# Attention and FFN block on one core: three rounded matmuls a product against one fp32 matmul

## The reference

```python
n  = layernorm(x)
q  = rope((n @ Wq).reshape(b, n, 32, 8)); k, v = split(ctx @ Wkv); k = rope(k)
x  = x + softmax(q @ k.T / sqrt(8)) @ v @ Wout + bout
h  = layernorm(x)
route = sum of the two largest of (h @ gate_w)          # 8 columns
y  = relu(h @ up_w)**2 @ down_w + (h @ expert_weight) * route
out = x + (layernorm(y) * gamma + beta)
```

## Time and profile before

| | us |
|---|---|
| median of 3 runs | 251.4 |
| lowest and highest run | 251.2, 253.0 |
| span of the profiled execution | 250.5 |
| TensorE matmuls busy in it | 221.1, 1754 records |
| VectorE, ScalarE, GpSimd busy | 167.7, 141.3, 105.3 |

### The profile page before, as it was taken

One profiled execution on the slowest core, in us unless ns is written; L12 is line 12 of the kernel. 1 busy time (PEld: TensorE's weight loads), 2 busy tenths in 40 slices (PEclk: granted clock), 3 DMA queues, 4 the chain that ended last, 5 costly groups with the idle time before them and its releaser, 6 DMA issues.

```text
span 250.5 us, 4919 instructions
## 1 busy us (share of the span) xinstructions
PE 221.1 (88%) x1754; PEld 175.5 (70%) x1754; DVE 167.7 (67%) x374; ACT 141.3 (56%) x284; POOL 105.3 (42%) x129
## 2 busy tenths in 40 slices
PE   2959768899999999999998999998889999778980
PEld 1847535677777787879786878877557886567980
DVE  6965899868886789684559974745998100572455
ACT  3256457597767675865647667564446967111520
POOL 7774566731238014474653136231324454332003
PEclk9995799999999999999999999999999999955896
DMA  7943141102101101010101110101000000000001
GB/s 199 357 94 84 47 107 45 28 20 62 48 24 29 42 3 48 0 48 0 47 0 43 46 47 0 46 3 44 0 27 21 5 0 3 0 0 22 3 21 42
DMA packets 12743, 10.68 MB, mean 43 GB/s; under 512 B 2992, under 2 KB 12336, under 8 KB 12720
## 3 DMA queue, kind: packets, MB, share of 16 engines
q1 hardware_dynamic: 11680, 10.37, 14.7%
q10 hardware_dynamic: 1040, 0.01, 0.2%
HBM read 5.13 MB, written 1.05 MB: 25 GB/s over the span
## 4 chain that ended last, share of the span: by engine, by line
PE 68%; DVE 18%; issue 6%; ACT 3%; POOL 2%; DMA 1%; POOLq 0%; DVEq 0%; ACTq 0%
PE ps_bg L956 18%; PE ps_bg L939 11%; PE ps_st L1037 11%; PE ps_o L1053 10%; PE ps_s L1021 9%; PE ps_dn L1109 9%; DVE mneg L837 7%; DVE stats L702 2%; DVE mnat L844 1%; PE ps_st L972 1%; DMA pos_sb<-in_fside_BxSx 1%; DVE mnat L845 1%; DVE by_token L710 1%; ACT kmask L612 1%; DVE rot_c L766 1%
## 5 line engine op out<-in xcount | busy, mean ns | idle before, releaser
L837 DVE TENSOR_REDUCE mneg<-ps_s 128x2 f32<-128x512 f32 x128 | 84.6, 684 | 36.4 <-PE ps_s L1021 35.7
L641 ACT ACTIVATE probs<-ps_st 128x512 f32<-128x512 f32 x128 | 73.3, 595 | 26.4 <-PE ps_st L1037 26.1
L1037 PE MATMUL ps_st<-qstack,kmask 128*128 128x256 f32 x256 | 57.3, 308 | 0.5 <-ACT probs L641 0.4
L1021 PE MATMUL ps_s<-kmask,qstack 128*128 128x512 f32 x128 | 54.4, 428 | 3.1 <-DVE mneg L837 1.9
L1037 PEld LDWEIGHTS ps_st<-qstack,kmask 128*128 128x128 f32 x256 | 39.9, 189 | 15.1 <-issue 9.5
L473 POOL TENSOR_SCALAR var_eps<-mv 128x1 f32<-128x1 f32 (+1 forms) x20 | 7.1, 353 | 75.0 <-DVE mv L705 74.9
L1053 PE MATMUL ps_o<-probs,vaug 128*32 128x256 f32 x512 | 34.3, 385 | 0.0
L1021 PEld LDWEIGHTS ps_s<-kmask,qstack 128*128 128x128 f32 x128 | 25.1, 197 | 7.2 <-DVE mneg L837 5.2
L956 PE MATMUL ps_bg<-x2nT,up 128*128 128x256 f32 x192 | 27.3, 296 | 1.0 <-ACT x2nT L573 1.0
L956 PEld LDWEIGHTS ps_bg<-x2nT,up 128*128 128x128 f32 x192 | 26.1, 202 | 2.0 <-ACT moe L672 1.4
L1109 PE MATMUL ps_dn<-down,inner 128*128 128x256 f32 x192 | 25.4, 283 | 0.2 <-DVE inner L341 0.2
(11 more groups left out here) (109 smaller groups left out, 311.5 us busy)
## 6 DMA issues: line engine op xcount, KB each, us to landing
kmask<-kstack SPq DMA_DIRECT2D x60, 64.0 KB, 2.1
x_sb<-in_x SPq DMA_DIRECT2D x4, 256.0 KB, 6.6
whole<-in_L_ffn_down_w SPq DMA_DIRECT2D x4, 256.0 KB, 5.4
qstack<-mT SPq DMA_DIRECT2D x64, 4.0 KB
result<-y_fin SPq DMA_DIRECT2D x8, 128.0 KB, 1.7
c_sb<-in_ctx SPq DMA_DIRECT2D x4, 128.0 KB, 2.4
oT<-in_L_ffn_up_w SPq DMA_DIRECT2D x1, 512.0 KB, 5.5
y_fin<-in_L_ffn_up_w SPq DMA_DIRECT2D x1, 512.0 KB, 7.4
```

The source lines that it names most:

```text
L641: act.activation(probs[n % 2][:, i, :, :], ps_st[k % NST][:].rearrange("p (t n) -> p t n", t=T), ACT.Exp, scale=SCALE).then_inc(st_free, 1)
L837: dve.tensor_reduce(mneg[m % 2][:, t, n % 2, 2 * half:2 * half + 2], ps_s[(4 * n + k) % NS][:].rearrange("p (i k) -> p i k", i=2), AX.X, A ...
L1021: pe.matmul(ps_s[(4 * n + k) % NS][:], qstack[b % 2][:, g, t * P:(t + 1) * P], kmask[:, g, 2 * half:2 * half + 2, :], start=True, stop=Tru ...
L1037: ins = pe.matmul(ps_st[k % NST][:, t * N:(t + 1) * N], kmask[:, g, i, t * P:(t + 1) * P], qstack[b % 2][:, g, :], start=True, stop=True)
```

## The change

Every product with weights is made of single fp32 matmuls on the operands themselves. All high and low parts go, with the operations that make them and the semaphores between; the copies out of the banks are ScalarE's alone and write fp32 once. The square writes `inner` directly. Weights are loaded straight into their tiles, all at the start, and the first use of each on TensorE waits for its load. The list, its slots and the warm-ups stay. Scores and PV stay as they are.

```diff
-        wkv = sb("wkv", [P, 2, 1, 2 * D], f32r)
-        wout = sb("wout", [P, 2, KC, D], f32r)
-        up = sb("up", [P, 2, KC, F], f32r)
-        expert = sb("expert", [P, 2, KC, D + E], f32r)
-        down = sb("down", [P, 2, FT, D], f32r)
+        wq = sb("wq", [P, KC, D])
+        wkv = sb("wkv", [P, 1, 2 * D])
+        wout = sb("wout", [P, KC, D])
+        up = sb("up", [P, KC, F])
+        expert = sb("expert", [P, KC, D + E])
+        down = sb("down", [P, FT, D])
         bout_sb = sb("bout_sb", [P, D])
...
@@ -325,20 +308,11 @@
 
 
 
-        def squares(eng, e, j):
+        def squares(eng, b, j):
+            taken(eng, (f"up{j}", b))
+            inner_read(eng, b, j)
             h = whole[j % HB][:]
-            if e == ("up0", B - 1):
-                eng.wait_ge(h_ready, 4 * (B - 1))
-            taken(eng, e)
-            eng.tensor_tensor(h, h, h, ALU.mult).then_inc(square_ready, 1)
-
-        def lo_squares(eng, b, j):
-            k = 4 * b + j
-            eng.wait_ge(square_ready, k + 1)
-            eng.wait_ge(h_hi_ready, k + 1)
-            hi, lo = (inner[:, j % 2, part, :, :] for part in range(2))
-            inner_read(eng, b, j)
-            eng.tensor_tensor(lo, whole[j % HB][:], hi.bitcast(f32), ALU.subtract).then_inc(h_ready, 1)
+            eng.tensor_tensor(inner[:, j % 2, :, :], h, h, ALU.mult).then_inc(h_ready, 1)
 
...
@@ -382,38 +337,27 @@
                 ring = slice(b % 2 * T, (b % 2 + 1) * T)
                 sp.dma_start(c_sb[:, ring, :], cv[:, b * T:(b + 1) * T, :]).then_inc(ld_c[b], 16)
 
-            def load_down(j):
-                sp.dma_start(whole[j % HB][:], by_rows(down_w)[:, 2 * j:2 * j + 2, :]).then_inc(ld_down[j % HB], 16)
-
             def load_tokens(b):
                 tiles = slice(b * T, (b + 1) * T)
                 if b < 2:
                     load_context(b)
                 if b == 0:
-                    sp.dma_start(raw_kv, Wkv).then_inc(ld_wkv, 16)
+                    sp.dma_start(wkv[:, 0, :], Wkv).then_inc(ld_wkv, 16)
                 sp.dma_start(x_sb[:, tiles, :], xv[:, tiles, :]).then_inc(ld_x[b], 16)
 
             load_tokens(0)
-            sp.dma_start(raw_q, by_rows(Wq)).then_inc(ld_wq, 16)
+            sp.dma_start(wq[:], by_rows(Wq)).then_inc(ld_wq, 16)
             load_tokens(1)
-            for k in range(KC):
-                sp.dma_start(raw_up[k], up_w[k * P:(k + 1) * P, :]).then_inc(ld_up, 16)
-            sp.dma_start(raw_out[:], by_rows(Wout)).then_inc(ld_wout, 16)
-            for j in range(HB):
-                load_down(j)
+            sp.dma_start(wout[:], by_rows(Wout)).then_inc(ld_wout, 16)
+            sp.dma_start(expert[:, :, 0:D], by_rows(expert_w)).then_inc(ld_expert, 16)
+            sp.dma_start(expert[:, :, D:D + E], by_rows(gate_w)).then_inc(ld_expert, 16)
+            sp.dma_start(up[:], by_rows(up_w)).then_inc(ld_up, 16)
+            sp.dma_start(down[:], by_rows(down_w)).then_inc(ld_down, 16)
             for b in range(2, B):
                 load_tokens(b)
             for v, t in ((bout, bout_sb), (gamma, gamma_sb), (beta, beta_sb)):
                 sp.dma_start(t[:], v.rearrange("(a d) -> a d", a=1).broadcast_to((P, D))).then_inc(ld_vec, 16)
             for e in ORDER:
-                while later_loads and e[0] == "S" and 4 * e[1] + e[2] >= later_loads[0][0]:
-                    _, which, split, count = later_loads.pop(0)
-                    sp.wait_ge(split, count)
-                    if which == "expert":
-                        sp.dma_start(raw_expert[:, :, 0:D], by_rows(expert_w)).then_inc(ld_expert, 16)
-                        sp.dma_start(raw_expert[:, :, D:D + E], by_rows(gate_w)).then_inc(ld_expert, 16)
-                    else:
-                        load_down(which)
                 if e[0] == "V" and e[1] + 2 < B:
                     sp.wait_ge(bg_full, full(("cT", e[1])))
...
@@ -525,19 +461,9 @@
                     xv = x_sb[:, b * T:(b + 1) * T, :]
                     pool.tensor_tensor(xv, xv, beta_sb[:].unsqueeze(1).broadcast_to((P, T, D)), ALU.add)\
                         .then_inc(x2b_ready, 1)
-                elif piece_at(e) is not None:
-                    i = piece_at(e)
-                    raw, parts, _, done = PIECES[i]
-                    pool.wait_ge(piece_hi, i + 1)
-                    pool.tensor_tensor(parts(1), raw, parts(0).bitcast(f32), ALU.subtract)\
-                        .then_inc(done, 1)
-                elif what[:2] == "up":
-                    j = int(what[2])
-                    if b < B - 1:
-                        squares(pool, e, j)
                 elif what[0] == "h":
                     if b < B - 1:
...
@@ -773,38 +668,15 @@
                 before = [by_token_uses(t)[by_token_uses(t).index(e) - 1] for t in range(T) if e in by_token_uses(t)]
                 bg_read(dve, *before)
 
-            def lo_part(e, parts, tokens=slice(0, N)):
-
-                hi, lo = (parts[:, part, :, tokens] for part in range(2))
-                dve.wait_ge(hi_ready, SPLIT[e] + 1)
-                of = bg(e)[:, 0:hi.shape[1] * hi.shape[2]].rearrange("p (k n) -> p k n", n=hi.shape[2])
-                emptied(dve.tensor_tensor(lo, of, hi.bitcast(f32), ALU.subtract), e)
-
             for e in ORDER:
                 what, b = e[0], e[1]
                 if what == "cT":
-                    if b >= 1:
-                        dve.wait_ge(bg_full, full(("V", b - 1)))
-                    else:
+                    if b == 0:
                         angles_in_turns()
-                    lo_part(e, cT)
                 elif what == "xT":
-                    if b >= 1:
-                        dve.wait_ge(bg_full, full(("Q", b - 1)))
-                    lo_part(e, xnT)
                     if b == 0:
                         taken(dve, ("K", b))
                         stack_rows(dve, link, 0, b)
-                elif what[:2] == "aT":
-                    t = int(what[2])
-                    if b >= 1:
-                        bg_read(dve, (f"W{t}", b - 1))
-                    lo_part(e, attnT, slice(t * P, (t + 1) * P))
-                elif what[:3] == "x2T":
-                    t = int(what[3])
-                    if b >= 1:
-                        bg_read(dve, ("E1", b - 1), ("up3", b - 1))
-                    lo_part(e, x2nT, slice(t * P, (t + 1) * P))
                 elif what == "ln1a":
                     dve.wait_ge(ld_x[b], 16)
                     if b >= 1:
...
@@ -940,29 +808,21 @@
                     at += m
                 ins.then_inc(bg_full, 1)
 
-            def split_product(to, lhs, rhs, fresh):
-
-
-
-                of, in_rhs = fresh
-                early, late = (((0, 0), (1, 0)), (0, 1)) if in_rhs else (((0, 0), (0, 1)), (1, 0))
-                terms = [(k, a, b_) for k in range(len(lhs)) for a, b_ in early]
-                terms += [(k, *late) for k in range(len(lhs))]
-                for c, (k, a, b_) in enumerate(terms):
-                    if c == 0:
-                        pe.wait_ge(hi_ready, SPLIT[of] + 1)
-                    if (a, b_) == late and k == 0:
+            def product(to, lhs, rhs, of):
+
+                for k in range(len(lhs)):
+                    if k == 0:
                         taken(pe, of)
-                    ins = pe.matmul(to, lhs[k][a], rhs[k][b_], start=(c == 0), stop=(c == len(terms) - 1))
+                    ins = pe.matmul(to, lhs[k], rhs[k], start=(k == 0), stop=(k == len(lhs) - 1))
                 return ins
 
-            def split_by_token(e, lhs, rhs, kc, cols, fresh):
+            def product_by_token(e, lhs, rhs, kc, cols, of):
 
                 begin(e)
                 for t in range(T):
-                    ins = split_product(bg(e)[:, t * D:(t + 1) * D],
-                                        [[lhs[:, a, k, t * P:(t + 1) * P] for a in range(2)] for k in range(kc)],
-                                        [[rhs[:, a, k, cols] for a in range(2)] for k in range(kc)], (fresh, False))
+                    ins = product(bg(e)[:, t * D:(t + 1) * D],
+                                  [lhs[:, k, t * P:(t + 1) * P] for k in range(kc)],
+                                  [rhs[:, k, cols] for k in range(kc)], of)
                 ins.then_inc(bg_full, 1)
 
             def keep_warm(count):
...
@@ -1067,32 +927,33 @@
                 elif what[0] == "W":
                     t = int(what[1])
                     if b == 0:
-                        pe.wait_ge(weights_split, WS)
+                        pe.wait_ge(ld_wout, 16)
                     begin(e)
-                    split_product(bg(e)[:, 0:D],
-                                  [[attnT[:, a, k, t * P:(t + 1) * P] for a in range(2)] for k in range(KC)],
-                                  [[wout[:, a, k, :] for a in range(2)] for k in range(KC)],
-                                  ((f"aT{t}", b), False)).then_inc(bg_full, 1)
+                    product(bg(e)[:, 0:D],
```

(75 more changed lines are left out.)

64 lines of the change are left out of this document (16 added, 48 removed).

## The result

The changed kernel takes 259.5 us (259.1 to 259.8) against 251.3 before (248.3 to 253.0). The ratio, between executions of comparable clock, is 1.037, interval 1.027 to 1.046. It is slower, as forecast (261.0, range 255 to 266). The runs of the kernel before spread by 5 us, those of the changed one by 1; TensorE's clock in the last batch is a part of the reason and its clock in the start another, as the experiments show.

A forecast was written before the change was run, and what follows sets the result against it. TensorE's queue was taken as the bound from 45 to 216 us, latencies outside it. The terms 7.1 - 0.6 + 3.2 = +9.7 took the span from 250.5 to 260.2, plus 0.9 gave 261 us, range 255 to 266.

The forecast's parts named there:

- Price of a product: On TensorE, 256 columns: 0.434 us as fp32 against 0.355 as three rounded matmuls, +0.079 at full clock.
- The two ends of the bounds: Limits on a product's price on TensorE: 0.236 us (-0.119 each) up to 0.65 us (+0.30 each).
- rival 2: Faster: at full array width fp32 records stream like rounded ones, 0.236 us a product, about 235 us in all; chance 0.07.
- rival 3: Weight loads on TensorE not hidden: +0.30 us on each of 141 products, +42, near 300 us; chance 0.03.
- (a): 45 to 216 us: 141 products cost +11.1 us, less 4.0 for waits and empty time on TensorE, sum +7.1.
- rival 1: Absorbed: TensorE's empty time and the other engines' relief take most of the cost; +3.4, 254.8 us; chance 0.17.
- (b): 0 to 45 us: dearer first products against low parts and weight pieces dropped; sum -0.6, between -2.5 and +1.
- So that is worth 0: Start: first K product ready about 2 us sooner, counted as no gain because the chain runs over the tokens.
- Rival 4: Start: the clock's rise near 11 us comes a stretch later, slowing Q and fifteen warm-ups; +3.3, 264.5 us; chance 0.07.
- (c): 216 us to the end: dearer products sum to +3.85, taken as +3.2 because the clock might rise earlier.
- From span to time: End of the sum: measured time taken as 0.9 us above the span, so 260.2 became 261.1.
- The signs named: Profile checks: 192 TensorE records fewer, spacing 0.217, VectorE 14 us less busy, ScalarE 17, GpSimd 31, attention 7 later, tail 37.

The follow-up runs named there:

- the repeated run: The changed kernel run again with no edit, for comparison on the same chip as the follow-up kernels: 259.4 us, ratio 1.039 to the kernel before.
- price-only kernel: Kernel before with each three-term product made one fp32 matmul on the high parts, low parts still made and waited for but unused: 264.0 us, ratio 1.046.

## Why the prediction was right, and where it was off

The direction and the mechanism are as forecast: TensorE was the full engine and pays more per product.

- Price of a product: 0.079 forecast, 0.077 measured (0.432 less 0.355). The two ends of the bounds are both out: full width streams no faster than the strips of L1053 (rival 2), and the weight loads stay hidden (rival 3). Of the two rules of the Trainium skill weighed there, the four passes of FP8 and Floating Point Precision, TensorE Precision Notes, are the one that these records bear out: a product is 0.432 / 0.118 = 3.7 times a rounded matmul. The 0.43 there isn't four times the rounded spacing at full clock, which would be 0.47; it is four times half of the 0.213 at the low clock.
- (a) The middle: +7.1 forecast, from 11.1 of price and 4.0 off; +7.0 measured, from 10.5 and 3.5 off. The terms are each 0.5 to 0.6 too large and cancel. What the relief took off was in good part empty time (5.1 to 2.9 us); with the helpers as before 1.0 us of the price did vanish, a small part of what rival 1 needs: it had +3.4 in all, and the times are 8.2 apart.
- (b) The start: -0.6 forecast, +1.1 measured in the profile (-0.2 in the repeated run, -0.5 in the changed kernel with tail warm-ups, whose start is the same). The step that failed is the one that puts the first weights' subtractions on GpSimd at nothing, "So that is worth 0": the subtraction for Wq, which it doesn't name, kept the memset away from VectorE's short operations, and without it these took 1.59 and 1.94 us and the tokens came later. With the memset moved the start gains 1.5 (by the medians) to 3.4 us (in the profile), so the relief was sized too small as well. That the forecast of -0.6 lies among the measured ones is luck: a relief too small and a stall left out. Rival 4 came in part: the spacing of the records fell to that of the full clock near 15.4 us, not near 11.1, the tokens' transposes having started 1.5 us later, and Q's eight records took 2.83 us (the windows give a granted clock of 1.00 there all the while, so this is read from the spacing alone); by 46 us most of that was made up.
- (c) The tail: +3.2 forecast, -1.2 measured (+0.6 in the repeated run, with 3.4 us of low clock). It is made of two things, and both were mis-sized. The low clock, which I carried over and gave 2.5 us at most, was gone; with warm-ups on both sides it is 33.8 against 32.4, +1.4. And of the price at full clock, 40 x 0.077 = 3.1, 1.7 didn't come, where I had counted 0.3. The price-only kernel, its tail at full clock too, is 34.6 us there, so 34.6 - 32.4 = 2.2 of the price come with the helpers as before, and 34.6 - 33.7 = 0.9 is relief; these are single executions.
- From span to time I kept 0.9 us; the profiled execution of the changed kernel lies 2.0 above its span, and that made up for part of a span forecast 2.8 too long (260.2 against 257.4). So the total, 261 against 259.5, came out nearer than its terms: the middle by its mechanism, the rest by errors of +1.7 in the start, -4.4 in the tail and +1.1 here that cancel in part.
- The signs named: 1562 records, spacing 0.216, GpSimd 30.5 less, VectorE 14.9. ScalarE's 14.5 is short of 17.5, since copies in a row overlap. The attention ended 8.1 us later, for 7; the tail was 33.7 us, not 37.

## What to carry to other kernels

When one engine is full, price a change by its records alone, spacing by spacing; on the full stretch here that came out to 0.1 us with the others relieved, and their relief was worth a quarter to a third of it. Where work is taken off an engine, look at what moves up in its queue: the next thing may collide with a neighbour, as a memset did here. And compare tails at equal clock: a few transposes in idle slots were worth about a percent in the kernel before (2.9 us) and 1.0 us in the denser one, so a part of the difference between the two was the clock and not the work.

## What was not expected of the hardware

- A GpSimd memset of 1.80 us stretched VectorE's copies and scalar operations within this memory from 0.18 us to between 1.6 and 1.9, in each kernel in which the two met; operations with sources in the matmul banks and sums of two inputs were not touched.
- The clock at the end: TensorE busy 12.3 of 16.5 us after 216 us went with 0.60 of full clock in the kernel before; in short holes filled with transposes (13.1 of 16.5) it stayed at 1.00, and in the changed kernel it stayed there without them. Why it did in the latter stays open: in the 3.4 us behind the last attention product, at full clock in both, TensorE is as busy in one as in the other (1.63 us before, 1.64 changed), and another execution of the changed kernel had 3.4 us at 1.2 GHz.
